# Another order for the last iteration of a mixture-of-experts loop: three blocks finish in the middle, and the fourth takes the last two turns

## What is computed

```python
def expert_step(acc, xs):
    w_gu, w_d, c_e = xs
    gu = x @ w_gu.T
    g, u = jnp.split(gu, 2, axis=-1)
    h = jax.nn.silu(g) * u
    acc = acc + h @ w_d.T * c_e[:, None]
    return (acc, None)
out, _ = jax.lax.scan(expert_step, jnp.zeros_like(x), (gate_up_proj, down_proj, combine.T))
...
x = _layernorm(x + _L0_ffn_ref(x, ...), axis=-1)
```

## Time and profile before

| What | us |
| --- | --- |
| Median of three runs | 892.55 |
| The runs | 892.3, 892.55, 893.52 |
| The profiled execution, its own time | 894.03 |
| Its span, first to last instruction | 892.1 |
| Last iteration, from about | 773 |
| Last matmul of the last down product, modelled end | 878.55 |

### The profile page before, as it was taken

One profiled execution on the slowest core, in us unless ns is written; L12 is line 12 of the kernel. 1 busy time (PEld: TensorE's weight loads), 2 busy tenths in 40 slices (PEclk: granted clock), 3 DMA queues, 4 the chain that ended last, 5 costly groups with the idle time before them and its releaser, 6 DMA issues.

```text
span 892.1 us, 14708 instructions
## 1 busy us (share of the span) xinstructions
PE 849.6 (95%) x5720; PEld 668.3 (75%) x5720; DVE 629.9 (71%) x1379; ACT 280.2 (31%) x502; POOL 143.6 (16%) x122
## 2 busy tenths in 40 slices
PE   8999999998999989999799989999999999999994
PEld 6966677776777768777477878788888888888873
DVE  3566787888878888779687765766565666566647
ACT  5431243212422034211443522333322333233232
POOL 2024301333013330134340400300000000000021
PEclk9999999999999999999899999999999999999997
DMA  9310000100001000000230014110212020000001
GB/s 331 125 37 1 1 2 1 48 1 18 1 1 48 7 11 1 1 24 4 85 103 1 25 38 145 44 55 2 87 48 65 0 88 29 29 1 1 1 24 71
DMA packets 12685, 35.82 MB, mean 40 GB/s; under 512 B 1488, under 2 KB 2384, under 8 KB 12112
## 3 DMA queue, kind: packets, MB, share of 16 engines
q1 hardware_dynamic: 12624, 34.98, 11.4%
HBM read 30.33 MB, written 2.36 MB: 37 GB/s over the span
## 4 chain that ended last, share of the span: by engine, by line
PE 81%; DVE 11%; issue 4%; ACT 2%; POOL 1%; DMA 0%; ACTq 0%; DVEq 0%; POOLq 0%
PE ps L246 20%; PE ps L247 19%; PE ps L248 19%; PE ps L1419 6%; PE ps L1499 5%; PE ps L1490 2%; PE ps L1293 2%; PE ps L1475 1%; PE ps L1329 1%; DVE small L1095 1%; DVE h_lo L348 1%; DVE su L511 1%; DVE xT_lo L960 1%; PE ps L1358 1%; PE ps L1286 1%
## 5 line engine op out<-in xcount | busy, mean ns | idle before, releaser
L511 DVE TENSOR_TENSOR su<-sg,ps 128x512 f32<-128x512 f32 x96 | 66.0, 687 | 132.8 <-PE ps L248 131.6
L246 PE MATMUL ps<-y_hi,f_hi 128*128 128x512 f32 x384 | 151.1, 394 | 0.0
L248 PE MATMUL ps<-y_hi,f_lo 128*128 128x512 f32 x384 | 149.5, 389 | 0.0
L247 PE MATMUL ps<-y_lo,f_hi 128*128 128x512 f32 x384 | 149.4, 389 | 0.0
L375 ACT ACTIVATE sg<-ps 128x512 f32<-128x512 f32 x96 | 57.3, 598 | 258.1 <-PE ps L248 258.1
L739 POOL TENSOR_TENSOR roped<-prod 128x512 f32<-128x512 f32 x64 | 80.9, 1285 | 170.2 <-DVE prod L1040 170.2
L1040 DVE TENSOR_TENSOR prod<-ps,ropeq 128x512 f32<-128x512 f32 x128 | 79.4, 682 | 27.1 <-PE ps L248 26.5
L246 PEld LDWEIGHTS ps<-y_hi,f_hi 128*128 128x128 f32 x384 | 72.2, 188 | 15.3 <-issue 0.5
L247 PEld LDWEIGHTS ps<-y_lo,f_hi 128*128 128x128 f32 x384 | 72.2, 188 | 15.3 <-issue 0.5
L248 PEld LDWEIGHTS ps<-y_hi,f_lo 128*128 128x128 f32 x384 | 72.1, 188 | 15.1
L246 PE MATMUL ps<-xT_hi,a_hi 128*128 128x512 f32 x192 | 78.4, 408 | 3.7 <-DVE xT_lo L960 3.7
(11 more groups left out here) (160 smaller groups left out, 1328.7 us busy)
## 6 DMA issues: line engine op xcount, KB each, us to landing
cb<-routing SPq DMA_DIRECT2D x32, 256.0 KB
f_raw<-in_L_ffn_gate_up_proj SPq DMA_DIRECT2D x8, 768.0 KB, 6.1
f_raw<-in_L_ffn_down_proj SPq DMA_DIRECT2D x8, 384.0 KB, 7.0
xb<-in_x SPq DMA_DIRECT2D x4, 512.0 KB, 4.6
lq<-in_L_xattn_Wq SPq DMA_DIRECT2D x1, 2048.0 KB, 16.2
x2T_all<-in_L_xattn_Wo SPq DMA_DIRECT2D x1, 2048.0 KB, 12.1
x2T_all<-x2T SPq DMA_DIRECT2D x4, 512.0 KB, 3.3
out<-res SPq DMA_DIRECT2D x4, 512.0 KB, 2.6
```

The source lines that it names most:

```text
L246: pe.matmul(dst, l_hi, r_hi, start=first, stop=False, skip_group_check=check)
L247: pe.matmul(dst, l_hi, r_lo, start=False, stop=False, skip_group_check=check)
L248: return pe.matmul(dst, l_lo, r_hi, start=False, stop=last, skip_group_check=check)
L511: dve.tensor_tensor(su[:, k % 2], sg[:, k % 2], bank(2 * (k % 2) + 1), ALU.mult).then_inc(s_su, 1)
```

## The change

Only the last iteration is changed.

- The turns go (0,0), (0,1), (0,2), (1,0), (1,1), (1,2), (0,3), (1,3). The second group of weights is needed from step 9 on, not 12; ACT splits it in steps 2 to 4, DVE in steps 3 to 8.
- `turn_out` of blocks 0, 1, 2 follows steps 15, 18, 21. Statistics stand in DVE's steps 15, 18, 22; the scale chains in steps 16 and 19, block 2's behind the steps. `final_apply` of blocks 0 and 1 stands in ACT's steps 17 and 20. Blocks 0 to 2 share PSUM banks 4 and 5, block 3 takes 0 and 1.
- GpSimd makes `lo` of the steps 14 to 21; DVE makes `lo(22)` in step 23 and `lo(23)` behind the steps.
- The last sum, the last transposes and the last store are made in halves of 256 tokens each.

```diff
+    LAST_ORDER = ((0, 0), (0, 1), (0, 2), (1, 0), (1, 1), (1, 2), (0, 3), (1, 3))
...
-    f_hi_step = lambda w, first: (20 if first else 14) if w == 0 else 4
-    f_lo_step = lambda w: 15 if w == 0 else 5
+    f_hi_step = lambda w, first, last: (20 if first else 14) if w == 0 else 2 if last else 4
+    f_lo_step = lambda w, last: 15 if w == 0 else 3 if last else 5
...
-    FINAL_BANKS = (4, 4, 0, 2)
-    POOL_STEP = 17
-    FINAL_STEP = 18
+    FINAL_BANKS = (4, 4, 4, 0)
+    POOL_STEPS = range(14, 22)
+    TURN_OUT_STEPS, STATS_STEPS, SCALE_STEPS, APPLY_STEPS = (15, 18, 21), (15, 18, 22), (16, 19, 23), (17, 20)
...
         for n in range(BLOCKS):
-            sp.wait_ge(s_res, TILES * (n + 1) - 2 * (n == LAST))
             if n == LAST:
                 sp.wait_ge(s_res_end, 2)
-            sp.dma_start(out[n], res[:, n]).then_inc(s_out, 16)
-        sp.wait_ge(s_out, 16 * BLOCKS)
+                sp.dma_start(out[n, :, 2:4], res[:, n, 2:4]).then_inc(s_out, 16)
+                sp.wait_ge(s_res, TILES * n + 2)
+                sp.dma_start(out[n, :, 0:2], res[:, n, 0:2]).then_inc(s_out, 16)
+            else:
+                sp.wait_ge(s_res, TILES * (n + 1))
+                sp.dma_start(out[n], res[:, n]).then_inc(s_out, 16)
+        sp.wait_ge(s_out, 16 * (BLOCKS + 1))
...
-                dve.tensor_tensor(acc[:, :, cols(n)], acc[:, :, cols(n)], ps[:, 6:8, :], ALU.add).then_inc(s_acc, 1)
+                halves = 2 if last and nb == NB - 1 else 1
+                for i in range(halves):
+                    s = slice(i * BT // halves, (i + 1) * BT // halves)
+                    a = acc[:, :, n * BT + s.start:n * BT + s.stop]
+                    dve.tensor_tensor(a, a, ps[:, 6:8, s], ALU.add).then_inc(s_acc, 1)
...
-                if (not first or k >= 1) and not (last and k > POOL_STEP):
+                if last and k == POOL_STEPS[-1] + 2:
+                    dve.wait_ge(s_hlo, base + k - 1)
+                if (not first or k >= 1) and not (last and k - 1 in POOL_STEPS):
                     lo(k - 1)
...
-                if last and k in (FINAL_STEP + 1, FINAL_STEP + 2):
-                    final_norm(0, k - FINAL_STEP - 1)
-                if last and k == FINAL_STEP + 4:
-                    final_norm(1, 0)
+                if last and k in STATS_STEPS:
+                    final_norm(STATS_STEPS.index(k), 0)
+                if last and k in SCALE_STEPS[0:2]:
+                    final_norm(SCALE_STEPS.index(k), 1)
             if last:
-                final_norm(1, 1)
-                final_norm(2, 0)
+                lo(STEPS - 1)
+                final_norm(2, 1)
                 accumulate(NB - 1)
-                final_norm(2, 1)
                 final_norm(3, 0)
                 final_norm(3, 1)
...
-                if last and k == FINAL_STEP:
-                    turn_out(0)
-                if last and k == FINAL_STEP + 3:
-                    turn_out(1)
+                if last and k in TURN_OUT_STEPS:
+                    turn_out(TURN_OUT_STEPS.index(k))
             if last:
                 dn(STEPS - 2)
-                turn_out(2)
                 dn(STEPS - 1)
                 turn_out(3)
```

More of the change, by code:

```diff
@@ L345, in h_lo_out @@
             eng.wait_ge(s_d, done - 2)
-        if eng is nc.gpsimd and k == POOL_STEP:
+        if eng is nc.gpsimd and k == POOL_STEPS[0]:
             eng.wait_ge(s_hlo, done)
@@ L387, in body @@
                     cT_out(act, LAST)
-                if 4 <= k < 7:
-                    if k == 4:
+                part = k - f_hi_step(1, first, last)
+                if 0 <= part < 3:
+                    if part == 0:
                         act.wait_ge(s_fload[1], it * 32 + 32)
-                    f_hi_out(act, 1, k - 4)
-                part = k - f_hi_step(0, first)
+                    f_hi_out(act, 1, part)
+                part = k - f_hi_step(0, first, last)
                 if 0 <= part < 3 and not last:
@@ L398, in body @@
                     f_hi_out(act, 0, part)
-                if last and k == FINAL_STEP + 3:
-                    final_apply(0)
+                if last and k in APPLY_STEPS:
+                    final_apply(APPLY_STEPS.index(k))
             if last:
                 hi(STEPS - 1)
-                final_apply(1)
                 final_apply(2)
@@ L422, in ffn_pool @@
             f_lo_part(pool, 0, 2, part)
-        for k in range(POOL_STEP, STEPS):
+        for k in POOL_STEPS:
             h_lo_out(pool, (GROUPS // 2 - 1) * STEPS + k, k)
@@ L497, in accumulate @@
             def accumulate(nb):
-                w, n = turn_of(nb, first)
+                w, n = turn_of(nb, first, last)
                 if first and w == 0 and n == LAST:
@@ L507, in body @@
                     accumulate((k - 5) // ROWS)
-                w, n, j = place(k, first)
+                w, n, j = place(k, first, last)
                 dve.wait_ge(s_sg, base + k + 1)
@@ L513, in body @@
                     dve.wait_ge(s_cb[w][n], it * 16 + 16)
-                if last and k >= POOL_STEP + 2:
+                if last and k - 2 in POOL_STEPS:
                     dve.wait_ge(s_hlo, base + k - 1)
@@ L549, in ffn_vector, with ffn_up @@
         over_groups(dve, body)
-    def ffn_up(pe, it, k, first):
+    def ffn_up(pe, it, k, first, last=False):
         base = it * STEPS
-        w, n, j = place(k, first)
+        w, n, j = place(k, first, last)
         f = 2 * (k % 2)
@@ L600, in turn_out @@
                                           acc[:, m, c:c + P], ident[:])
-                mm.then_inc(s_ft, 1)
+                    if t == TILES - 1 or n == LAST and t == 1:
+                        mm.then_inc(s_ft, 1)
             for k in range(STEPS):
                 if not first or k >= 2:
-                    ffn_up(pe, it, k, first)
+                    ffn_up(pe, it, k, first, last)
                     dn(k - 2)
```

24 lines of the change are left out of this document (13 added, 11 removed).

## The result

The changed kernel takes **898.9 us** (median of 7 runs, 896.33 to 900.74) against 892.55 for the kernel before (7 runs beside them, 892.21 to 894.06). The ratio, taken from all runs and not from the two medians, is 1.0061, with a 95% interval of 1.0050 to 1.0073: slower, by 5.5 us or 0.6%. The forecast was 897.9 us with a range of 894.6 to 900.0. The profiled execution took 898.61 us, with a span of 896.8.

A forecast was written before the change was run, and what follows sets the result against it. TensorE, 95% busy, was taken to bound the kernel until the last down product, then DVE's queue. Terms of 6.75 - 3.15 + 0.05 = +3.65 us gave 896.2, plus 1.7 for one clock fall 897.9 us; range 894.6 to 900.0.

The forecast's parts named there:

- Weights of the second group: Before step 9's gate, PE waits for DVE's sixth piece of low weights, now made in step 8: +1.5 us.
- The sums behind the chains: Steps 16 and 19: DVE's sums stand behind scale chains, so dn(15) and dn(18) start 3.0 us late each: +6.0 us.
- The hold: Steps 16 and 19: GpSimd's low half holds up DVE's scale chain, making dn(15) 2.9 us late instead of 1.8.
- The waits of before that go: PE's old waits in step 20 and before block 1's transposes vanish, with their restarts: -1.4 us.
- The end of the steps: DVE now makes lo(22) behind hc(23), so PE takes dn(22) later: +0.65 us.
- Behind the last down product: DVE's cleared queue lets block 3's statistics start 2.0 us after that product instead of 5.15: -3.15 us.
- The store: Block 3's store in two halves: the second lands at most 0.34 us later; taken as +0.05 us.
- The sum: All terms before the clock: 6.75 - 3.15 + 0.05 = +3.65 us, a median of 896.2 us.
- The clock: Behind the two new long PE waits, one fall to half clock was counted, 1.7 us: 896.2 becomes 897.9 us.
- Both waits cost the clock: Rival: the clock falls behind both new waits for x2T_all, giving 899.6 us; chance 0.25.
- No hold: Rival: GpSimd does not delay the scale chains; both waits 1.8 us, no clock fall, 894.0 us; chance 0.08.
- The sums come in time: Rival: DVE's sums end before dn(15) is due, the 6.0 us go, 890.2 us; chance 0.06.

The follow-up runs named there:

- experiment 1: The changed kernel with DVE splitting the second group's low weights in steps 2 to 7 instead of 3 to 8: 899.62 us.
- experiment 5: The changed kernel with 11 unread matmuls ahead of each of dn(15) and dn(18), and DVE's second-group weights one step earlier: 895.47 us.
- experiment 3: The changed kernel with DVE instead of GpSimd making low halves 16 and 19, so GpSimd runs nothing beside the scale chains: 895.11 us.
- experiment 2: The changed kernel with the sums ahead of the scale chains in steps 16 and 19, nothing else: 890.57 us.
- experiment 10: The kernel of experiment 7 with the last block stored by one whole transfer instead of two halves: 886.25 us.
- experiment 7: The changed kernel with weights one step earlier, last-iteration sums first, lo(22) on GpSimd, and the first iteration's third sum ahead of routing work: 886.04 us.

## Why the prediction was right, by its steps

- **Weights of the second group, +1.5.** Measured: the wait is 1.28 and the restart 0.08 in the row's width and 0.16 before it, 1.5 in all. Experiments 1 and 5 take it away by splitting the weights one step earlier.
- **The sums behind the chains, +6.0.** Measured: twice 2.75, with 0.16 and the restart of 0.08 each, 6.0. The hold was the step with one row behind it; experiment 3 gives 1.05 to 1.08 for it where the working took 1.1, and experiment 2 shows that the order is what exposes it.
- **The waits of before that go, -1.4.** None of the two is left; 0.21 in step 23 stayed, for 0.23.
- **The end of the steps, +0.65.** Measured: a wait of 0.43, with 0.16 and a restart of 0.11 it is 0.7.
- **Behind the last down product, -3.15.** Measured: 5.15 - 1.93 = 3.22.
- **The store, +0.05.** Measured: 3.1 from issue to end in both kernels, so 0.0; experiment 10 agrees. The rule of the Trainium skill weighed there (DMA: Bandwidth & Descriptors, Anatomy of one DMA) would have had the end come 0.26 us sooner; that section fits it to transfers issued by GpSimd, and these are issued by SyncE. No run shows the 0.26, and the measurement decides: in experiments 7 and 10 the halves take about 0.1 us more from first issue to end, not less.
- **The sum.** Put together from measured terms it is 1.5 + 6.0 - 1.4 + 0.7 - 3.2 = +3.6 us, where the prediction had 3.65. It can be held against the two profiles. PE comes to the gate of step 9 at 809.16 - 1.28 - 0.16 = 807.72, where it came at 809.75 before. These 2.0 us, all ahead of the first wait that the change makes, are the 0.56 seen at 508 us and a fall in the first iteration that only the profiled execution of before had. With the two falls of 3.2 behind the new waits, 892.1 - 2.0 + 3.6 + 3.2 = 896.9, and the span is 896.8.
- **The clock** is the term that was mis-sized, and it carries the 1.0 us between 897.9 and 898.9. The price of a fall was right (1.63 and 1.60 for 1.7). The number was not: the profiled execution had two falls behind the new waits, as in the rival *Both waits cost the clock*. The base was wrong too, the other way: 892.55 is one number for two groups of runs, some with the first iteration's fall and some without. An estimate from the lower group of before, 891.8: with the 3.6 and no fall a run takes 895.4 us, with one 897.0, with two 898.6, with three 900.2. The profiled execution is known to have two and took 898.61; the median, 898.9, is next to it, and the seven runs, 896.33 to 900.74, reach from about one fall to three. So the forecast took about one fall too few (1.6) on a base about 0.7 too high, and part of its closeness is luck. The same mixture is the likely reason why the medians are 6.35 us apart and the ratio says 5.5. The places do not fall together, as the profiles show (the change: behind both new waits and not in the first iteration; experiment 1: behind the second new wait alone; experiment 3: in the first iteration alone), and the changed kernel's seven runs spread over 4.4 us where before's seven spread over 1.9. How often each place falls was not measured: seven runs and one profile don't tell it.
- **The rivals.** "No hold" is out by the widths above. "The sums come in time" is what experiment 2 makes true, at 890.57 where the working gave 890.2.

## What to carry to other kernels

In an in-order queue, an operation that frees another engine's buffer goes ahead of a chain of small dependent ones: here two moved lines turned a loss of 0.6% (5.5 us) into a gain of 0.3% (about 2.9 us) over the kernel before, and the same move in the first iteration gave 2 us more. When work is cleared from the end of a program, price what it displaces in the steps it moves to, including what a neighbouring engine does in them. And look at the single times before trusting a median: two groups with a gap may mean one wait that sometimes costs the clock and sometimes not.

## What the runs showed of the hardware that was not expected

- A wait of the same length costs the clock in one execution and not in another. Behind the wait of 2.42 us at 523 us the clock was 0.53 in the profile of before and 1.00 in that of the change; behind the 2.75 us at 848 it was 0.50 in the change and 1.00 in experiment 1. Behind the waits of 1.70 and 1.67 us in experiment 3 it did not fall, in the one profile that was taken. What decides it in a given execution no run here shows.
- In experiment 1 the clock was down before PE worked again: 0.97 for 862 to 864, with the wait ending at 864.45.
- In these rows a small DVE operation that reads two inputs from SBUF, and that starts while GpSimd's low half runs, ends 0.02 us after it: 0.16 us became 1.23 and 1.20 in the change, and 1.14 in the earlier trace rows. One that reads PSUM was not held: in experiment 3 `su` starts at 843.82 beside GpSimd's operation of 843.59 to 844.88 and is 0.69 us wide, as elsewhere. The prediction counted on it from that one row; experiment 3 shows that it goes when GpSimd's operation goes. The Trainium skill (SBUF — State Buffer, Who interferes with whom) says that a DVE instruction with two SBUF inputs contends with a GpSimd one that reads SBUF, since they share a pair of ports, and that the order of issue decides who blocks. The trace agrees, in all three rows.
